# A mixture-of-experts stage with its row work one place earlier in each step and half of its weight splits half a tile earlier

## What is computed

```python
# x, ctx: 8 sequences x 512 tokens x 512 features, float32
x = x + attention(layernorm(x), ctx, ctx, 16 heads)
flat = layernorm(x).reshape(4096, 512)
scores = softmax(flat @ router_weight.T + router_bias)          # 8 experts
w = scores of the 2 largest experts of each token, 0 elsewhere
gu = einsum('th,ehf->tef', flat, gate_up_proj) + gate_up_bias
gate = minimum(gu[..., :512], 7); up = clip(gu[..., 512:], -7, 7)
act = (up + 1) * gate * sigmoid(1.702 * gate)
x = x + einsum('teh,te->th', act @ down_proj + down_bias, w)
```

## Time and profile before

| what | value |
|---|---|
| median of 3 runs | 2020.74 us (2017.11 to 2023.55) |
| the profiled execution, its own time | 2016.04 us |
| its span in the profile | 2014.3 us |
| TensorE busy | 1766.2 us, 88% of the span |
| VectorE busy | 1365.4 us, 68% |
| ScalarE busy | 666.7 us, 33% |
| GpSimd busy | 513.8 us, 26% |
| mean granted TensorE clock | 0.942 of full |

### The profile page before, as it was taken

The page is one execution under the profiler, slowest core; times in us unless marked ns, Lnnn a source line. Parts: engine busy times, 40 slices in busy tenths (PEclk is TensorE's granted clock), DMA queues, the critical chain, the costliest instruction groups (busy, mean ns, idle before and its releaser), DMA issues. The chain is left out here.

```text
span 2014.3 us, 31367 instructions
## 1 busy us (share of the span) xinstructions
PE 1766.2 (88%) x10597; PEld 1279.7 (64%) x10597; DVE 1365.4 (68%) x2488; ACT 666.7 (33%) x1107; POOL 513.8 (26%) x628
## 2 busy tenths in 40 slices
PE   6989999999899998998995489989888897889896
PEld 4547456375474563744733378878787787878785
DVE  3776766767766667577576776766776777667764
ACT  2341532523415325144161222323233324233221
POOL 3113022021130221211310103333333334243332
PEclk9999999999999999999997589989998899899998
DMA  6405216034061150430601502535254425434322
GB/s 212 114 1 168 64 43 188 2 114 119 1 177 55 56 176 2 136 96 1 166 24 45 178 22 85 184 97 182 95 182 146 161 87 200 164 113 168 106 85 74
DMA packets 103798, 216.06 MB, mean 107 GB/s; under 512 B 25937, under 2 KB 26961, under 8 KB 103633
## 3 DMA queue, kind: packets, MB, share of 16 engines
q1 hardware_dynamic: 75696, 135.27, 21.2%
q0 software_dynamic: 27936, 78.73, 13.0%
HBM read 204.19 MB, written 37.36 MB: 120 GB/s over the span
## 5 line engine op out<-in xcount | busy, mean ns | idle before, releaser
L1265 PE MATMUL gu_ps<-xgT_hi,wg_hi 128*128 128x256 f32 x1248 | 370.6, 297 | 108.5 <-issue 108.5
L1265 PE MATMUL gu_ps<-xgT_lo,wg_hi 128*128 128x256 f32 x1248 | 365.7, 293 | 0.0
L1265 PE MATMUL gu_ps<-xgT_hi,wg_lo 128*128 128x256 f32 x1248 | 365.2, 293 | 0.0
L1265 PEld LDWEIGHTS gu_ps<-xgT_hi,wg_hi 128*128 128x128 f32 x1248 | 253.4, 203 | 124.2 <-issue 124.2
L448 ACT ACTIVATE pt<-st 128x1024 f32<-128x1024 f32 x256 | 249.3, 1018 | 152.3 <-PE st L291 152.3
L1265 PEld LDWEIGHTS gu_ps<-xgT_lo,wg_hi 128*128 128x128 f32 x1248 | 253.5, 203 | 0.0
L1265 PEld LDWEIGHTS gu_ps<-xgT_hi,wg_lo 128*128 128x128 f32 x1248 | 252.5, 202 | 0.0
L1496 POOL DMA_INDIRECT out<-acc,idx x78 | 133.2, 1707 | 368.2 <-DVE acc L1410 356.3
L609 DVE TENSOR_REDUCE negmax<-work 128x1 f32<-128x512 f32 x256 | 175.0, 689 | 62.5 <-PE work L276 61.3
L1325 ACT ACTIVATE sig<-gate 128x256 f32<-128x256 f32 x156 | 65.2, 418 | 359.5 <-DVE gate L1373 354.9
L1373 DVE TENSOR_SCALAR gate<-gu_ps,bg 128x256 f32<-128x256 f32 x156 | 75.5, 484 | 158.6 <-PE gu_ps L1265 123.4
(11 more groups left out here) (195 smaller groups left out, 3197.5 us busy)
## 6 DMA issues: line engine op xcount, KB each, us to landing
raw_g<-w_gate_up SPq DMA_DIRECT2D x39, 2048.0 KB
raw_d<-w_down SPq DMA_DIRECT2D x39, 1024.0 KB
ks<-k_hi SPq DMA_DIRECT2D x256, 64.0 KB, 2.1
qs<-q_hi SPq DMA_DIRECT2D x256, 64.0 KB, 2.4
bd<-b_down SPq DMA_DIRECT2D x39, 256.0 KB
x_in<-x SPq DMA_DIRECT2D x8, 1024.0 KB, 5.4
ctxT<-ctx_t SPq DMA_DIRECT2D x8, 1024.0 KB, 5.7
ks<-k_lo POOLq DMA_DIRECT2D x128, 64.0 KB, 2.4
```

The lines of the kernel that those rows point to most:

```text
L1265: ins = e.matmul(gu_ps[n % GU_BANKS][:, part, :], wg[s][pw][:, k, cols], xgT[s][px][:, k, :], start=(k == 0 and m == 0), stop=(k == KD - 1 ...
```

## The change

Five edits are made in the expert stage, and the arithmetic stays as it was.

1. On TensorE `turn_rows(i+2)` moves from between `gate_up(i+1)` and `down(i)` to the head of step i.
2. On ScalarE `row_hi(i+2)` moves from the end of step i to its head. On VectorE `row_lo(i+2)` and `pick_weight(i+2)` move from the end of the step to behind `clip(now, 0)`.
3. The four gate_up splits of a tile, which were spread over the step before its use (one in each f), are moved. Parts 0 and 1 of tile i+3 are done at the end of step i; parts 2 and 3 of tile i+2 are done early in step i, on ScalarE both ahead of the first sigmoid, on VectorE at f = 0 and f = 1. The down splits move on VectorE from f = 1 and 3 to f = 2 and 3.
4. In `mix` the bias pass of half j comes right behind the product pass of half j, and the wait for the bias stands first.
5. GpSimd issues `fetch(i+3)` ahead of `store_sums(i-1)`. For this there are 6 index buffers in place of 4 and 4 weight buffers in place of 3.

```diff
@@ -1167,7 +1167,7 @@
     KD, KF = D // P, F // P
     SUB = FTOK // P
     GU_BANKS = 4
-    IDX, WSL = 4, 3
+    IDX, WSL = 6, 4
     DX = D + E
     rows = xln_dram.rearrange("b s d -> (b s) d")
     out_rows = out.rearrange("b s d -> (b s) d")
@@ -1282,10 +1282,10 @@
 
             turn_rows(0)
             for i in range(-1, n_tiles):
+                if i + 2 < n_tiles:
+                    turn_rows(i + 2)
                 if i + 1 < n_tiles:
                     gate_up(i + 1)
-                if i + 2 < n_tiles:
-                    turn_rows(i + 2)
                 if i >= 0:
                     down(i)
 
@@ -1336,25 +1336,29 @@
             row_hi(0)
             for i in range(-1, n_tiles - 1):
                 now = i + 1
+                if i + 2 < n_tiles:
+                    row_hi(i + 2)
                 if i >= 0:
                     down_hi(i + 1, changed_flag(e, i + 1))
                 else:
                     e.wait_ge(raw_d_in[0], 16)
                     for k in range(KF):
                         d_hi(e, 0, k)
-                changed = None
+                    changed = changed_flag(e, 1)
+                    for k in range(KD // 2):
+                        gate_up_hi(1, k, changed)
                 if i + 2 < n_tiles:
-                    changed = changed_flag(e, i + 2)
-                    gate_up_hi(i + 2, 0, changed)
+                    for k in range(KD // 2, KD):
+                        gate_up_hi(i + 2, k, changed)
                 for f in range(KF):
                     gate_sigmoid(now, f)
                     if f:
                         hidden_hi(now, f - 1)
-                    if f + 1 < KF and changed is not None:
-                        gate_up_hi(i + 2, f + 1, changed)
                 hidden_hi(now, KF - 1)
-                if i + 2 < n_tiles:
-                    row_hi(i + 2)
+                if i + 3 < n_tiles:
+                    changed = changed_flag(e, i + 3)
+                    for k in range(KD // 2):
+                        gate_up_hi(i + 3, k, changed)
 
         def on_dve(e):
             def row_lo(i):
@@ -1400,12 +1404,11 @@
                 s = i % 2
                 e.wait_ge(acc_in[s], turn(i) * 16 * SUB)
                 e.wait_ge(w_made.sem, w_made[i, "slot"])
+                e.wait_ge(bd_in[s], turn(i) * 16)
                 for j in range(SUB):
                     e.wait_ge(down_made.sem, down_made[i, j])
                     e.scalar_tensor_tensor(out=acc[s][:, j, :], in0=d_ps[j][:, :], scalar=w_slot[i % WSL][:, j:j + 1], in1=acc[s][:, j, :],
                                            op0=ALU.mult, op1=ALU.add).then_inc(y_added.sem, 1)
-                e.wait_ge(bd_in[s], turn(i) * 16)
-                for j in range(SUB):
                     e.wait_ge(y_added.sem, y_added[i, j])
                     e.scalar_tensor_tensor(out=acc[s][:, j, :], in0=bd[s][:, :], scalar=w_slot[i % WSL][:, j:j + 1], in1=acc[s][:, j, :],
                                            op0=ALU.mult, op1=ALU.add).then_inc(mixed.sem, 1)
@@ -1436,33 +1439,37 @@
                 gu_lo(e, 0, k)
             row_lo(0)
             pick_weight(0)
-            for i in range(-1, n_tiles):
+            changed = changed_flag(e, 1)
+            for k in range(KD // 2):
+                gate_up_lo(1, k, changed)
+            for i in range(-1, n_tiles - 1):
                 now = i + 1
-                if now < n_tiles:
-                    down_changed = changed_flag(e, now)
-                if i + 2 < n_tiles:
-                    changed = changed_flag(e, i + 2)
-                if now < n_tiles:
-                    e.wait_ge(bg_in[now % 2], turn(now) * 16)
-                    e.tensor_scalar(bu1[now % 2][:, :], bg[now % 2][:, KF:], 1.0, None, ALU.add).then_inc(bu1_made.sem, 1)
-                    for f in range(KF):
-                        if f > 1:
-                            hidden_lo(now, f - 2)
-                        clip(now, f)
-                        if f:
-                            glu(now, f - 1)
-                        if f == 1 and i >= 1:
-                            mix(i - 1)
-                        if f % 2:
-                            down_lo(now, f // 2, down_changed)
+                down_changed = changed_flag(e, now)
+                e.wait_ge(bg_in[now % 2], turn(now) * 16)
+                e.tensor_scalar(bu1[now % 2][:, :], bg[now % 2][:, KF:], 1.0, None, ALU.add).then_inc(bu1_made.sem, 1)
+                for f in range(KF):
+                    if f > 1:
+                        hidden_lo(now, f - 2)
+                    clip(now, f)
+                    if f:
+                        glu(now, f - 1)
+                    if f < 2:
                         if i + 2 < n_tiles:
-                            gate_up_lo(i + 2, f, changed)
-                    glu(now, KF - 1)
-                    hidden_lo(now, KF - 2)
-                    hidden_lo(now, KF - 1)
-                if i + 2 < n_tiles:
-                    row_lo(i + 2)
-                    pick_weight(i + 2)
+                            gate_up_lo(i + 2, KD // 2 + f, changed)
+                    else:
+                        down_lo(now, f - 2, down_changed)
+                    if f == 0 and i + 2 < n_tiles:
+                        row_lo(i + 2)
+                        pick_weight(i + 2)
+                    if f == 1 and i >= 1:
+                        mix(i - 1)
+                glu(now, KF - 1)
+                hidden_lo(now, KF - 2)
+                hidden_lo(now, KF - 1)
+                if i + 3 < n_tiles:
+                    changed = changed_flag(e, i + 3)
+                    for k in range(KD // 2):
+                        gate_up_lo(i + 3, k, changed)
             mix(n_tiles - 2)
             mix(n_tiles - 1)
 
@@ -1500,11 +1507,10 @@
             fetch(1)
             fetch_sums(0)
             for i in range(-1, n_tiles):
-                if i >= 1:
-                    store_sums(i - 1)
                 if i + 3 < n_tiles:
                     fetch(i + 3)
                 if i >= 1:
+                    store_sums(i - 1)
                     fetch_sums(i)
             store_sums(n_tiles - 1)
             e.wait_ge(scattered.sem, scattered[n_tiles - 1])
```

## The result

The changed kernel takes 2036.61 us (median of 4, 2034.04 to 2038.08), and the kernel before 2019.97 in the same runs: ratio 1.008, 95% interval 1.006 to 1.0101. It is slower by 0.8%, where the forecast was 2001.5 and faster. The profiled execution has a span of 2036.4 us.

What follows compares the result with a forecast made beforehand. TensorE was bound by gaps ahead of gate_up, put down to late row splits behind ScalarE's weight waits. Stage -11, start -6.6, end -1.6 make -19 us: 2001.5 us from a median of 2020.74, range 1982 to 2023.

Steps and rivals of the forecast that it cites:

- Start: Before the expert stage's second tile: gate_up(1) starts at 1166.1 in place of 1172.72, 6.6 us earlier.
- Floor: Quiet steps (no new weights): 18.02 us each, 37 times, with the small gap of 0.73 to 0.8 us ahead of gate_up gone.
- End: Last three tiles, scatter, gather and mix: the scatter no longer waits for the second product pass, 1.6 us won.
- A changed pair: Two neighbouring tiles with new weights: 17.1 us over the floor, seven times; TensorE's gap moves from gate_up to down and grows.
- Load: landing took 9.45 us: Replay of a changed pair: raw_g, issued at 13.7 us after gate_up(5) starts, lands 9.45 us later, at 23.15.
- In step 8 VectorE has caught up: Step behind the first changed pair: mix(6) frees its first half near 79.6, down(7) comes at 82.6; no excess counted.
- ScalarE's wait for `raw_d` is gone: Sign expected in the profile after: ScalarE no longer waits for raw_d; its waits for raw_g come twice a pair.
- second held step: Second tile of a changed pair: down(6) starts 7.1 us late, waits 0.8 more, 2.2 of half clock; excess 10.2 us.
- The length of VectorE's queue: VectorE's work in a changed pair between the landing and mix, named as the step trusted least.
- the gap is dearer through the clock: Rival at down of the two held steps: half clock runs on, 3.9 us more a pair, 2029 us; chance 0.12.
- The fetch ahead: GpSimd's fetch(i+3) ahead of the scatter: worth nothing, since no quiet or changed step waited for the rows.
- both loads land together: Rival on the second landing of a pair: raw_g lands with raw_d at 12.2 us, 2020.5 us, no change; chance 0.14.

Runs made afterwards that it cites:

- e9: Changed kernel with one more wait on GpSimd, so the four gathers of the next sums are issued later: 2000.92 us, ratio 0.9908.
- e10: Changed kernel with both scatters waiting for the mix's last pass, its passes still alternating: 2013.79 us, ratio 0.9966.
- e3: Changed kernel with mix's passes in their old order, both product passes and then both bias passes: 2004.18 us, ratio 0.9931.
- e4: Changed kernel with mix's passes in their old order and the fetch behind the scatter again: 2082.75 us, ratio 1.0322.
- e8: Kernel before with only SyncE's down bias load put behind the raw_g load: 2030.02 us, ratio 1.0044.
- e11: Kernel before with only the mix of a tile moved to the end of VectorE's own step, behind the row work: 1913.76 us, ratio 0.948.
- e6: Changed kernel with mix(i) moved to the end of VectorE's step i, ahead of the splits that wait for raw_g: 1865.53 us, ratio 0.9232.

## Why the prediction was wrong

From the predicted span of 1995.2 to the measured 2036.4 us are 41 us. By the prediction's own terms:

- **Start**: predicted gate_up(1) at 1166.1, measured 1166.67. Right (+0.6).
- **Floor**: 17.85 in place of 18.02, 37 times: -6.3. The small gap is gone as forecast.
- **End**: 42.7 us before, 40.0 after gate_up(38): -2.7 in place of -1.6.
- **A changed pair**: 829.7 - 37 x 17.85 = 169 us above the floor, where 7 x 17.1 + 1.2 = 121 were forecast: +48. This is the step that failed. Its 7.1 us a pair are 2.5 in the first step, 1.6 in the second and 2.9 in the third.

Within the pair, **the step that failed is "Load: landing took 9.45 us"**, a duration taken from a trace in which other transfers stood elsewhere; it was 11.16 in the mean. With it failed "In step 8 VectorE has caught up" and "ScalarE's wait for `raw_d` is gone": the third step pays 2.9 us and ScalarE waits 37.4 us in all for `raw_d`. In the kernel before, the first gather was issued 2.15 us behind `raw_g` (1262.63 and 1264.78 in its timeline); in the changed one it goes 0.16 us ahead of it. The alternating passes finish the first half of the sums sooner, its scatter goes sooner, and the gathers behind the scatters meet `raw_g` on the same DMA engines. I replayed every engine's queue but GpSimd's, and priced the alternating passes by VectorE alone (0.2 us). With the gathers held back (e9), 37 steps take 790.6 us against the 788 of the prediction, and the kernel 2000.92 against 2001.5. That agreement is partly luck: the floor is 6 us lower, and with fewer gathers in it than in the kernel before a landing is 8.70 us, not 9.45. The cause is shown by e9, which delays the gathers alone. That the alternating passes bring it about by way of the scatter is shown by e10 and agrees with e3.

By steps: the first held step was predicted at 6.9, is 6.7 in e9 and 9.4 in the changed kernel. The third was predicted at 0, is 0.0 in e9 and 2.9 in the changed kernel. There ScalarE stands 5.08 us for `raw_d`, which took 9.64 us beside the gathers; VectorE's row split, which needs nothing of `raw_d`, stands 4.71 us. It waits its turn behind ScalarE's count for splits that are skipped in this tile. ScalarE's sequencer gives that count (L1310) only once it is past the wait for `raw_d`, and the waits of the kernel after name it in five of the seven pairs:

```profile
DVE xgT_lo L1369 <- ACTq L1310: 22.8, 5, 6.3
```

In e9, where `raw_d` lands in 5.5 us, this wait is 3.9 us in all and the step costs nothing. The kernel before had a third gap too, 2.77 us ahead of the gate_up at 1339.21, which the prediction did not count:

```profile
1339.21 0.55 PE L1265 MATMUL gu_ps<-xgT_hi,wg_hi 128*128 128x256 f32 x1 [2.77 <-issue]
```


The **second held step** is 11.8 to 11.9 in both, against 10.2: a mis-sized term. The prediction had ScalarE reach `raw_d` 12.5 us after the issue of `raw_g` and wait for nothing. It landed 14.86 us after it in the changed kernel (1279.37 to 1294.23) and 14.91 in e9 (1276.03 to 1290.94), whatever the order of the gathers, with 285 and 284 GB/s moved over those windows. All of `raw_g`, `raw_d` and the gathers, 4.2 MB, comes in by then in both. The 12.2 us of the kernel before had 4.1 MB in them, at 339 GB/s, 0.23 MB of that the end of the scatter; so the bytes are again only a part of the difference, and the rest is open. Whether gathers put behind `raw_d` too would shorten this was not tried.

**The length of VectorE's queue**, the step I trusted least, held: 10.2 us from landing to `mix` predicted, 9.74 measured. So did the interval from `mix` to the next `raw_g` (2.95 predicted, 3.45 measured).

**The clock** was a smaller part of the error. Windows of the kernel after, on the first `down`, the idle time ahead of the second, and the second (columns as in the earlier trace rows):

```profile
1273.83:1282.23 8.40, 8.40 (x30) 6.48 (x31) 7.21 (x16) 1.88 (x5) 4.44 (x6) 0.73 0.36 114
1294.00:1303.80 9.80, 0.05 (x2) 0.03 (x1) 6.68 (x14) 5.22 (x9) 0.00 (x0) 0.75 0.00 0
1303.80:1312.70 8.90, 8.90 (x32) 6.91 (x33) 8.58 (x18) 1.67 (x4) 4.93 (x6) 0.70 0.40 120
```

After 5.7 us of idle TensorE the next 8.4 us were granted 0.73, after 9.8 us the next 8.9 us 0.70; that is about 2.3 + 2.7 = 5.0 us of clock in this pair. Of a pair's 24.2 us 18.4 are waits and 5.8 the rest, mostly clock (predicted 3.65). In e9 it is 13.9 of waits and 4.7. The rival "the gap is dearer through the clock" gave nearly the right time (2029) for a reason that carries some 2 of the 7.1 us a pair.

**The fetch ahead, "worth nothing"**, was wrong by 78.6 us (e3 against e4), and so was "If it were undone, the rows of tile i+3 would still have most of a step". With turning first, the rows of a tile are wanted at the head of the step, and fetched behind the scatter they came up to 8.9 us late. The error does not show in the total only because the change has the part that cures it.

**The reading of the kernel before** was wrong too. I put its gaps down to ScalarE's waits for `raw_g` and `raw_d`. e8 takes those waits away and the gaps stay within 0.8 us in the first pair; e11 takes the mix out of the chain ahead of the row split and 107 us go. ScalarE's wait was nearly all covered; VectorE's queue, with the mix in its middle, was the bound.

The Trainium skill ("DMA: Bandwidth & Descriptors", Queues, rings and completion order) says under arbitration that a DMA engine which has work on several queues goes round between them, packet by packet. The trace agrees. In the microsecond from 1258.85 of the kernel after, in the midst of `raw_g`, both queues move about as much:

```profile
q1 hardware_dynamic: 55, 0.23, 54.9%
q0 software_dynamic: 59, 0.19, 46.9%
```

I had weighed that section for the order of `raw_g` and `raw_d` in one queue, not for this. On those two the rows follow its ring order: in e9 `raw_g` is there at 1284.36 and `raw_d`, issued 1.90 us behind, at 1290.94, so the rival "both loads land together" did not occur.

## What to carry to other kernels

When a change frees a buffer sooner, follow the queue that waits for the buffer to the transfers it will issue, and set them beside the loads that the critical engine waits for. A landing time read from a trace belongs to the traffic of that trace. Here the gathers, issued 3.7 us sooner than in e9 (first gather against `raw_g`), put 0.7 MB more ahead of the end of each 2 MB load and about 1 MB beside the 1 MB load of the third step, and cost 36 us.

Before moving work ahead of a wait, ask what a wait moved ahead of other work will hold. The splits half a tile sooner put a wait for 2 MB ahead of the mix, which frees PSUM, lets the scatter go and, through the bias load on SyncE, lets the next 2 MB be asked for: a loop in which each late landing delays the next. With the mix ahead of those splits (e6) the whole loop of 170 us is gone.

When TensorE waits for the end of a chain of two engines, test which link binds before naming one. An engine that stands at its queue's head may still be early.

## What the runs showed that was not expected

A 2 MB load landed, from its issue to ScalarE's start, in 8.70 us in the mean with no gather issued in its first 3 us and in 11.16 with the first of four gathers issued within 0.5 us of it. For the 1 MB load it was 5.5 and 9.4 us (means of 7). Being issued first did not put the gathers first: in the first pair their packets begin 4.6 us behind the issue of `raw_g`, 4.8 us behind their own, and `raw_g` has the engines to itself until then:

```profile
q1 hardware_dynamic: 218, 0.89, 92.1%
```

This is SyncE's queue from 1253.85 to 1256.85 in the kernel after; GpSimd's moved nothing in it.

One wait more on an engine that had time (e9) made the kernel 1.8% faster. The changed kernel's own order, with the mix moved (e6), is 7.7% faster than before; the same move in the old order (e11) gives 5.2%.
